# A bias as rows of the keys, a causal mask as three rows and four diagonal products, and one root for a norm of a norm

## Time and profile before

| | us |
|---|---|
| median of 3 runs | 2062.75 (2059.64 to 2069.62) |
| the profiled execution | 2063.91 |
| its span | 2062.1 |
| PE busy | 1650.3 (80%) |
| PE weight load | 1071.9 (52%) |
| DVE busy | 1209.1 (59%) |
| ACT busy | 1042.4 (51%) |
| POOL busy | 686.4 (33%) |

### The profile page before, as it was taken

How to read it: one execution, slowest core, us unless ns; L and a number is a source line. 1 busy time by engine, 2 the same in 40 slices (tenths; PEclk the granted TensorE clock), 3 DMA queues, 4 the chain that set the end, 5 groups by cost and what they waited for, 6 DMA issues and landing times. The chain is left out here.

```text
span 2062.1 us, 42577 instructions
## 1 busy us (share of the span) xinstructions
PE 1650.3 (80%) x14902; PEld 1071.9 (52%) x14902; DVE 1209.1 (59%) x3694; ACT 1042.4 (51%) x2171; POOL 686.4 (33%) x1196
## 2 busy tenths in 40 slices
PE   1788997999998999868998996667577688788544
PEld 0333444677665666544444665555344477676332
DVE  3454555544436889845887655454665542366666
ACT  1344443433325777644554563534344565486556
POOL 4343310120003333212555312731667430541460
PEclk9995558999997999978999998888755698898756
DMA  7544426630005555331222211353745122321100
GB/s 198 127 92 110 120 58 184 205 82 1 0 1 125 127 133 142 73 111 44 68 64 62 75 49 63 91 143 96 191 100 129 57 67 71 107 87 39 45 26 21
DMA packets 191504, 184.65 MB, mean 90 GB/s; under 512 B 26528, under 2 KB 174944, under 8 KB 189984
## 3 DMA queue, kind: packets, MB, share of 16 engines
q1 hardware_dynamic: 182288, 145.22, 27.1%
q10 hardware_dynamic: 816, 19.92, 3.2%
q0 software_dynamic: 8192, 16.79, 2.9%
HBM read 119.67 MB, written 80.74 MB: 97 GB/s over the span
## 5 line engine op out<-in xcount | busy, mean ns | idle before, releaser
L2209 DVE TENSOR_REDUCE mneg<-psb 128x4 f32<-128x512 f32 (+1 forms) x576 | 383.3, 684 | 206.2 <-PE psb L1803 198.7
L2583 ACT ACTIVATE HB<-psb 128x512 f32<-128x512 f32 x384 | 218.7, 596 | 147.5 <-PE psb L1803 143.5
L1803 PE MATMUL psb<-K,Q 48*128 48x128 bf16 (+1 forms) x1280 | 192.5, 265 | 114.0 <-DMA Q<-sc_q 44.5
L1803 PE MATMUL psb<-Q,K 51*128 51x128 bf16 (+2 forms) x1664 | 267.2, 301 | 5.5 <-ACT HB L2583 2.3
L2802 POOL TENSOR_SCALAR rs<-mv 128x2 f32<-128x2 f32 (+1 forms) x96 | 21.9, 229 | 654.7 <-DVE mv L2169 652.4
L1803 PEld LDWEIGHTS psb<-K,Q 48*128 48x128 bf16 (+1 forms) x1280 | 111.8, 113 | 204.7 <-issue 134.6
L2583 ACT ACTIVATE HB<-psb,bias 128x512 f32<-128x512 f32 x192 | 131.2, 685 | 169.5 <-PE psb L1803 168.6
L1803 PEld LDWEIGHTS psb<-Q,K 51*128 51x128 bf16 (+2 forms) x1664 | 177.1, 138 | 29.7 <-issue 11.6
L1803 PE MATMUL psb<-HB,VA 128*9 128x128 f32 (+1 forms) x2560 | 164.0, 340 | 5.2 <-ACT OE L2588 4.7
L1803 PE MATMUL psb<-KS,Q 48*128 48x128 bf16 x1024 | 140.0, 228 | 25.6 <-DMA Q<-mT 11.3
L1803 PE MATMUL psb<-biasT,selbb 96*128 96x512 bf16 x192 | 109.9, 572 | 0.0
(11 more groups left out here) (480 smaller groups left out, 3816.6 us busy)
## 6 DMA issues: line engine op xcount, KB each, us to landing
K<-sc_k SPq DMA_DIRECT2D x96, 192.0 KB, 3.7
Q<-sc_q SPq DMA_DIRECT2D x96, 192.0 KB
tok_rows<-in_zero ACTq DMA_DIRECT2D x16, 1152.0 KB, 32.8
sc_q<-comp SPq DMA_DIRECT2D x48, 192.0 KB, 2.2
K<-tok_rows SPq DMA_DIRECT2D x72, 128.0 KB, 2.1
sc_q<-comp SPq DMA_DIRECT2D x48, 128.0 KB, 2.1
vraw<-in_ctx SPq DMA_DIRECT2D x48, 128.0 KB, 4.7
KS<-sc_s SPq DMA_DIRECT2D x32, 192.0 KB
```

What stands on the lines that cost most here:

```text
L1803: return pe.e.matmul(out, w, x, start=start, stop=stop, skip_group_check=True)
L2209: t = e.tensor_reduce(m.mneg[:, s.b % 4, s.i * A.per:(s.i + 1) * A.per], PSB[s.use.bank].rearrange("p (h k) -> p h k", h=A.per), AX.X, ALU ...
L2583: a.done(act(m.HB[:, s.slot, :], PSB[s.use.bank], ACT.Exp, bias=bz), s.use.drained)
```

## The change

Three things are changed, with the planner's costs for them.

The bias of A0: K8 gets three more rows a head in A0 (n_rows 51 instead of 48), which hold the three bf16 parts of the bias, and Q8 has ones there. The rows of the maxima move from 48..50 to 51..53. The bias rows are written once to DRAM behind each pair's key rows (`bias_store`, six DMAs), and three rows of zeros behind the query rows of A1 (three DMAs), so that `rows_load` brings 51 rows. The product with biasT and the bias of Exp go in A0; A2 keeps both. All four places of Q8 are set to one at the start. The nine DMAs of `bias_store` wait for biasT on SP.

The causal mask: rows 24 to 26 of KS and Q8 hold, for three of the four blocks of 32 tokens, a pair of rows whose product is -1e30 wherever the key's block lies behind the query's. What is left is the diagonal of 32 x 32 blocks, which four products of 32 rows, 32 columns and 128 streamed columns mask, in `scores` and in `weights`.

The norm of a norm: one root of var * (1 + eps) + eps^2 takes the place of two roots and the work between them.

```
-        "norm_in": ... {None: 2000 if s.rms else 1600, "second": 3200, "both": 4100}[s.twice])),
+        "norm_in": ... {None: 2000 if s.rms else 1600, "second": 3200, "both": 1900}[s.twice])),
-        "scores": ... (220 if A.bias_i is not None or A.causal else 0)), ("dve", 720)),
+        "scores": ... (100 if A.causal else 220 if A.bias_i is not None and not A.bias_rows or A.causal else 0)), ("dve", 720)),
-        "weights": ... (220 if A.causal else 0)), ...
+        "weights": ... (100 if A.causal else 0)), ...
...
+        self.longer = {n: nc.dram_tensor(n, [NP, 51 * 16, 256], BF16, kind="Internal").ap() for n in ("sc_k", "sc_q1")}
+        self.scratch |= {n: a[:, 0:768, :].rearrange("p (c q) t -> p c q t", c=6) for n, a in self.longer.items()}
...
-        self.n_rows, self.halves = (96, 1) if dh == 16 else (48, 2)
+        self.n_rows, self.halves = (96, 1) if dh == 16 else (51, 2)
+        self.bias_rows = bias_i is not None and dh != 16
...
     do("setup", cst=t_cst, ints=t_i, g=t_g, cols=t_cols, uses=biasu)
+    do("bias_store", need=t_biasT)
+    t_bias_rows = dma("dma_bias", 6)
+    t_zero_rows = dma("dma_zeros", 3)
...
-                do("ks_zero", A=AF, p=p, need=need)
+                do("ks_zero", A=AF, p=p, need=need, q_need=q8_free[AF.at(p)])
                 dma(f"dma_ks{AF.at(p)}", 2)
+                dma(f"dma_q8{AF.at(p)}", 2)
...
+    def diagonal(o4, way):
+        corner = m.cnegb[0:32, way, 0:32].unsqueeze(1).broadcast_to([32, 4, 32])
+        for i in range(4):
+            o = slice(32 * i, 32 * i + 32)
+            t = matmul(o4[o, :, o], m.identb[0:32, 0:32], corner, False, True, False)
+        return t
...
-        if A.bias_i is not None:
+        if A.bias_i is not None and not A.bias_rows:
             t = matmul(o4, m.selbb[:, s.b:s.b + 1].broadcast_to([96, 128]), ...)
         if A.causal:
-            t = matmul(o4, m.identb[:, :], m.cnegb[:, 0, :].unsqueeze(1).broadcast_to([128, 4, 128]), False, True, False)
+            t = diagonal(o4, 0)
...
         for i in range(2):
-            v.done(e.memset(m.place(m.K8, i), 1.0), ("clear_dve", i + 1))
+            v.done(e.memset(m.place(m.Q8, i), 1.0), ("clear_dve", 2 * i + 1))
+            v.done(e.memset(m.place(m.K8, i), 1.0), ("clear_dve", 2 * i + 2))
...
-        else:
+        elif s.twice != "both":
             then(e.tensor_scalar(r0, var, EPS, None, ALU.add))
-        if not s.twice:
+        if s.twice == "both":
+            then(e.tensor_scalar(r0, var, 1.0 + EPS, EPS * EPS, ALU.mult, ALU.add))
+        if s.twice != "second":
...
+    def bias_store(s):
+        sp.wait_ge(s.need)
+        rows = m.longer["sc_k"][:, 768:816, :].rearrange("p (c h) t -> p c h t", c=3)
+        zero = m.longer["sc_q1"][:, 768:816, :].rearrange("p (c h) t -> p c (h t)", c=3)
+        for c in range(3):
+            for b in range(2):
+                src = m.biasT[32 * c + b:32 * c + 32:2, 0, :].unsqueeze(1).broadcast_to([16, 16, 128])
+                load("bias", rows[:, c, :, 128 * b:128 * b + 128], src)
+        for c in range(3):
+            load("zeros", zero[:, c].bitcast(F32), io["zero"][0:16, :])
```

More of the change, by code:

```diff
@@ L102, in reckon @@
     f = {
-        "norm_in": lambda: (("dve", 450 * s.n), ("pool", {None: 2000 if s.rms else 1600, "second": 3200, "both": 4100}[s.twice])),
+        "norm_in": lambda: (("dve", 450 * s.n), ("pool", {None: 2000 if s.rms else 1600, "second": 3200, "both": 1900}[s.twice])),
         "norm_out": lambda: ((s.by, (380 if s.by == "dve" else 290) * s.norm.n),),
@@ L111, in reckon @@
         "v_copy": lambda: (("dve", 330),),
-        "scores": lambda: (("pe", (230 if not s.beside else 130) + (220 if A.bias_i is not None or A.causal else 0)), ("dve", 720)),
+        "scores": lambda: (("pe", (230 if not s.beside else 130) + (100 if A.causal else 220 if A.bias_i is not None and not A.bias_rows or A.causal else 0)), ("dve", 720)),
         "max_parts": lambda: (("dve", 1050),),
         "max_rows": lambda: (("pe", 130), ("act", 290), ("sp", 650 * A.halves)),
-        "weights": lambda: (("pe", (230 if not s.scores else 130) + (220 if A.causal else 0)), ("act", 640 if A.bias_i is None else 720)),
+        "weights": lambda: (("pe", (230 if not s.scores else 130) + (100 if A.causal else 0)), ("act", 640 if A.bias_i is None else 720)),
         "sums": lambda: (("pe", 560 * len(s.blocks)),),
@@ L674, in make_plan @@
     t_tg = inc("act", "tanh_gates")
-    k8_free[0], k8_free[1] = inc("dve", "clear_dve"), inc("dve", "clear_dve")
+    q8_free[0], k8_free[0], q8_free[1], k8_free[1] = (inc("dve", "clear_dve") for _ in range(4))
     t_const = inc("dve", "consts")
-    k8_free[2], k8_free[3] = inc("pool", "clear_pool"), inc("pool", "clear_pool")
+    q8_free[2], k8_free[2], q8_free[3], k8_free[3] = (inc("pool", "clear_pool") for _ in range(4))
     va_free[:] = [inc("pool", "clear_pool")] * 4
@@ L1849, in score_mask @@
         if A.causal:
-            t = matmul(o4, m.identb[:, :], m.cnegb[:, 0, :].unsqueeze(1).broadcast_to([128, 4, 128]), False, True, False)
+            t = diagonal(o4, 0)
         pe.done(t, s.use.full)
     def scores(s):
-        s["last"] = s.A.bias_i is None and not s.A.causal
+        s["last"] = (s.A.bias_i is None or s.A.bias_rows) and not s.A.causal
         if s.beside:
@@ L2751, in setup @@
     def setup(s):
-        ones(m.K8, 2, count())
-        ones(m.K8, 3, count())
+        for at in (2, 3):
+            ones(m.Q8, at, count())
+            ones(m.K8, at, count())
         g.wait_ge(before[0])
@@ L2814, in norm_in @@
         then(e.tensor_scalar(r0, r0, EPS, None, ALU.add))
-        if s.twice == "second" and s.by == "act":
+        if s.by == "act":
             then(e.tensor_tensor(r0, r0, power, ALU.pow))
             shift()
-        elif s.twice == "second":
+        else:
             done(e.tensor_tensor(r0, r0, power, ALU.pow), s.rstd)
[L2820 to L2826, removed]
     def split(s):
@@ L2898, in rows_load @@
         else:
+            rows = sc[p].rearrange("c (d h) t -> (c d) h t", d=A.dh)
+            if s.sc == "sc_q1" or s.sc == "sc_k" and A.bias_rows:
+                rows = m.longer[s.sc][p].rearrange("(r h) t -> r h t", h=16)
+            n = rows.shape[0]
             for half in range(2):
-                src = sc[p].rearrange("c (d h) t -> (c d) h t", d=A.dh)[:, 8 * half:8 * half + 8, :]
-                load(name, dst[64 * half:64 * half + 6 * A.dh, :].rearrange("r (h t) -> r h t", h=8), src)
+                load(name, dst[64 * half:64 * half + n, :].rearrange("r (h t) -> r h t", h=8), rows[:, 8 * half:8 * half + 8, :])
     def ks_zero(s):
-        sp.wait_ge(s.need)
-        for r in (24, 88):
-            load(f"ks{s.A.at(s.p)}", m.place(m.KS, s.A.at(s.p))[r:r + 24, :].bitcast(F32), io["zero"][:, 0:1024])
+        at = s.A.at(s.p)
+        sp.wait_ge(s.need, s.q_need)
+        for r in (24, 88):
+            load(f"ks{at}", m.place(m.KS, at)[r:r + 24, :].bitcast(F32), io["behind_k"])
+            load(f"q8{at}", m.place(m.Q8, at)[r:r + 3, :].bitcast(F32), io["behind_q"])
+    def bias_store(s):
+        sp.wait_ge(s.need)
+        rows = m.longer["sc_k"][:, 768:816, :].rearrange("p (c h) t -> p c h t", c=3)
[6 more added lines that the diff above has]
+            load("zeros", zero[:, c].bitcast(F32), io["zero"][0:16, :])
     def v_load(s):
@@ L3038, in layout @@
     a["zero"] = np.zeros((24, 2048), np.float32)
+    block = np.arange(128) // 32
+    behind = np.where(block[None, :] > np.arange(24)[:, None], np.float32(-1e30), np.float32(0))
+    behind[3:] = 0
+    own = (block[None, :] == np.arange(3)[:, None]).astype(np.float32)
+    for name, v in (("behind_k", behind), ("behind_q", own)):
+        bits = c(np.tile(v, (1, 16))).view(np.uint32)
+        a[name] = c(((bits + 0x8000) >> 16).astype(np.uint16)).view(np.float32)
     a["cols"] = c(np.concatenate([a.pop(name) for name, _ in COLS], axis=1))
```

12 lines of the change are left out of this document (6 added, 6 removed).

## The result

The changed kernel takes 2209.5 us (median of 4 runs, 2202.7 to 2214.9) against 2061.2 for the kernel before in the same comparison: ratio 1.072, 95% interval 1.066 to 1.079. It is slower by 148 us, where 76 less were forecast. The profiled execution took 2202.7 with a span of 2200.6, 138.5 us longer than the span of before.

What follows compares the result with a forecast made beforehand. PE was taken to bound A0 and AF, DVE A1. The terms -60 + 4 - 15 - 5 = -76 us against the profiled 2063.9 gave 1988, as a median 1987 us, with a range of 1957 to 2031.

Steps and rivals of the forecast that it cites:

- Part 1: A0: bias as key rows removes 128 products, 67 us of PE; stage -60 us, bounds -67 and -29.
- I take idle growing from 30.5 to 38: A0: PE's idle time grows only from 30.5 to 38 us, so the stage ends after about 201 us, -60.
- the feed takes the bound's place: Rival, chance 0.20: SyncE's queue holds each pair; A0 only -29 us, in all -34, 2029.
- Part 2: Price at the start, +4 us; three extra rows in loads of K (A0, A1) and Q (A1) are 6% of 192 KB each.
- Start, +4: Start: nine DMAs waiting for biasT stand ahead of the weight loads; between 1.4 and 10 us, taken as +4.
- Part 3: AF: small causal products take 0.33 us a pair instead of 0.54; -15 us, bounds -1 and -25.
- slower by draining: Rival, chance 0.04: AF's eight small products drain PE one by one; AF +97 us, in all +36, 2099.
- I count half: AF from 962 to 1112: DVE often later, so half the saving on some 74 units, 7.5 us.
- DVE has room: AF from 1124 to 1237: the full saving of 0.21 us on some 38 units, 8 us.
- the clock rises: Rival, chance 0.20: A0 without bias products gets a faster PE clock, DVE then bounds; A0 -81 us, in all -97, 1966.
- some us either way: Whole kernel: two planner costs change the order of steps; every stall may move by some us, carried by the range.
- Part 4: Tail: GpSimd's norm-of-a-norm pass falls from 4.32 to 2.07 us; -5 us, bounds 2.25 and 9.

Runs made afterwards that it cites:

- nobias: The kernel before with A0's 128 bias products left out and nothing in their place, planner cost of 220 dropped there too; ratio 0.992.
- full: The changed kernel with AF's causal mask again added by full products of 128x512 instead of four of 32x32; ratio 1.055 to the kernel before.
- split_full: The changed kernel with each 51-row load issued as 48 + 3 rows and the full 128x512 causal products; ratio 1.009 to the kernel before.
- split: The changed kernel with each load of 51 rows issued as two, of 48 and 3 rows; ratio 1.019 to the kernel before.
- early: split_full with the preparation of A0's next pair placed one pass over a batch earlier; ratio 1.014 to the kernel before.
- bonly: The kernel before with bias rows (48 + 3 rows a load) and the new norm of a norm, AF wholly as before; ratio 0.998.
- best: The kernel before with bias rows for A0 alone (48 + 3 a load, stored behind the weight loads) and the new norm, AF as before; ratio 0.996.
- rows52: best with each A0 key load in one piece of 52 rows (the 52nd zero) instead of 48 + 3; ratio 0.994 to the kernel before.
- other: rows52 with A0's pairs 2 to 15 loaded from the pair two before, ahead of their own stores (wrong rows); ratio 0.991 to the kernel before.
- caus: The kernel before with the change's causal mask alone (mask rows, four 32x32 products) and its planner cost of 100; ratio 1.033.
- norm: The kernel before with the change's norm of a norm alone (four GpSimd instructions for nine, planner cost 1900 for 4100); ratio 1.000.

## Why the prediction was wrong

The forecast was -76 us and the spans differ by +138.5: start +8.5, A0 +29, between A0 and A1 +1, A1 +56, AF +51, the rest -7.

*Part 1, A0 -60.* PE's saving was right: unit 1.09 us, busy time -63 in *nobias*. The forecast cut A0 at 305 us, though its last sums end near 327; to there before has 283 us and 34 of idle time, which changes nothing in the saving. The step that failed is "I take idle growing from 30.5 to 38". It grew to 75 with no cost at all in DMA. The rival *the feed takes the bound's place* had the mechanism and nearly the size (-29; -22 measured), and 0.20 was too little for it. The bound argued from the sum of idle time over the second half (6.5 us), where PE was so slow that it hid the feed. A period per pair, feed against PE, would have said it: PE is busy 15.6 us a pair in before (249 over 16) and 11.6 in *nobias* (186 over 16), and the forecast's own estimate of the feed, 14.5, lies between them. Measured, a pair of *nobias* takes 16.3 (261 over 16).

*Part 2, "the three extra rows ... are 6% of 192 KB each".* This is the costliest line: priced by bytes at nothing, they cost 4.6 points of the ratio (*full* 1.055 to *split_full* 1.009), 48 us in A0 and 56 in A1, which the forecast left out wholly. The number of rows sets how many engines share the load: 3 for 51 rows.

*Start, +4.* It is +8.5. The bias and zero rows' nine issues end at 24.00 and not at 22.8; the weights end at 33.63 and the first products begin at 52.53, and K's loads of 51 rows are slow there too. In the four versions with 48 + 3 rows and the bias rows still ahead of the weights (*split*, *split_full*, *early*, *bonly*) the first product is at 47.3 to 49.0, so that +4 for the issues was about right and the rest is the row count. SyncE's issues, then PE's first product with its idle time:

```profile
18.12 3.96 SPq L2865 DMA_DIRECT2D sc_k<-biasT  x6
22.12 1.87 SPq L2865 DMA_DIRECT2D sc_q<-in_zero  x3
...
33.68 1.70 SPq L2865 DMA_DIRECT2D sc_q<-comp  x3
```
```profile
52.53 1.03 PE L1813 MATMUL psb<-K,Q 51*128 51x128 bf16 x8 [28.47 <-DMA Q<-sc_q]
```

In *best* and *rows52*, with the bias rows behind the weights, A0 starts at 44.0 and 44.4, as before.

*Part 3, AF -15.* The price of the small products was right (0.33, 0.22), and the rival *slower by draining* was wrong. What failed is that the clock was taken as given: "I count half" and "DVE has room" held the unit at 2.4 GHz. Without the wide products the stage is at 1.2 GHz for most of its length (granted clock 0.61 to 0.70). That was asked for A0 (*the clock rises*), with the sign the other way, and never for AF. And the planner's cost, a constant beside the change, was waved through as "some us either way": it is 1.4% (0.5 to 2.2), some 29 us. The extra small loads are eight, of 0.26 to 0.30 us of issue each, not four; that is nothing beside the rest.

*Part 4, -5.* Right, as far as can be seen: 7 us of the difference between the spans.

*The rival "the clock rises in A0".* Not so: without the bias products (*nobias*) the granted clock from 155 to 305 us is 0.61 where it was 0.50; the rival had 0.95.

## What to carry to other kernels

Before adding a row to a load, look at the row count: 51 or 47 rows cost more than 52 or 48. Before taking work off the busiest engine, put its period beside that of its feed, per turn of the loop; the gain ends where they meet. And wide products may pay for the clock of all that stand beside them: price a stage at both clocks when its wide products go. A planner's costs are part of a change: try the new costs alone.

## What the runs showed of the hardware

One DMA engine moved 25 GB/s in these loads of 4 KB a row (share 0.06), three 76 (0.19). Cutting one row off a load of 48 made the kernel 18.6% slower. A write of row maxima let PE go on 2.00 to 2.08 us after its issue in 19 of 26 stalls of *other*. With PE busy 149.35 of 150 us the granted clock of AF was 0.50 in *caus*, from 962 to 1112 us; before has 144.37 busy and 1.00 there. The row of *caus*:

```profile
962.00:1112.00 150.00, 149.35 (x1597) 81.95 (x1596) 88.94 (x314) 65.84 (x151) 52.01 (x98) 0.50 0.17 47
```

The clock column shows 1.00 up to a trace's first record (at 76 to 319 us here, always a rise to 1.00), while spacings of 0.54 us for 512 columns show 1.2 GHz. In before the first record is at 138 us, and the column has 1.00 from 100 to 137:

```profile
100.00:137.00 37.00, 36.95 (x345) 15.23 (x341) 24.06 (x60) 17.44 (x31) 17.62 (x25) 1.00 0.36 81
```
```profile
121.45 0.61 PE L1803 MATMUL psb<-biasT,selbb 96*128 96x512 bf16 x1
121.99 0.62 PE L1803 MATMUL psb<-HB,VA 128*9 128x128 f32 x8
```

Early stages must be read by spacings, and the clock of A0 as a whole (0.71 before, 0.73 after) is too high in both. Where the kernel before took 2177 or 2190 us, AF and all behind it were longer, by 49 and 68 us in *norm* against before, and A0 and A1 were not.
